# First row tiles of a routed feed-forward loaded before the last four scatter sends

## What is computed

```python
normed = layernorm(x) * ln_gamma + ln_beta
probs = softmax(normed @ router_w.T)            # 8 experts
top_v, top_i = top_k(probs, 2)
gates = softmax(top_v)
for e in range(8):                              # swiglu, 128 -> 384 -> 128
    out += comb[:, e] * swiglu(normed, gate_up_w[e], down_w[e])
out += swiglu(normed, shared_gate_up_w, shared_down_w)
x = x + tanh(g_ffn[1]) * out
```

## Time and profile before

| | |
|---|---|
| median of 3 runs | 318.86 us (317.61 to 321.77) |
| the profiled execution's own time | 318.32 us |
| its span in the trace | 316.4 us |
| instructions | 7622 |
| PE busy | 273.7 us (87%) |
| DVE busy | 231.8 us (73%) |
| ACT busy | 207.7 us (66%) |
| POOL busy | 155.1 us (49%) |
| mean granted PE clock | 0.951 of full |

### The profile page before, as it was taken

The page is one execution under the profiler, slowest core; times in us unless marked ns, Lnnn a source line. Parts: engine busy times, 40 slices in busy tenths (PEclk is TensorE's granted clock), DMA queues, the critical chain, the costliest instruction groups (busy, mean ns, idle before and its releaser), DMA issues.

```text
span 316.4 us, 7622 instructions
## 1 busy us (share of the span) xinstructions
PE 273.7 (87%) x2454; PEld 207.2 (65%) x2454; DVE 231.8 (73%) x702; ACT 207.7 (66%) x481; POOL 155.1 (49%) x202
## 2 busy tenths in 40 slices
PE   8787996896999896999888763969899999999995
PEld 4463352455677554687666651348799999999995
DVE  4468178956987755788989967899577777777765
ACT  2765599986577678976864743534577777878530
POOL 2524289023632628625022778781027888888700
PEclk9899999999999999999999955589999999999999
DMA  7790002100349999980000111113212222201074
GB/s 210 228 362 39 1 2 85 48 3 0 134 151 190 182 189 182 190 130 0 2 1 11 35 36 43 51 51 84 57 52 79 71 77 70 68 32 37 8 233 135
DMA packets 34613, 28.13 MB, mean 89 GB/s; under 512 B 3072, under 2 KB 32389, under 8 KB 33936
## 3 DMA queue, kind: packets, MB, share of 16 engines
q1 hardware_dynamic: 32192, 23.77, 33.6%
q0 software_dynamic: 2240, 3.72, 3.6%
q10 hardware_dynamic: 144, 0.15, 0.2%
HBM read 14.15 MB, written 14.40 MB: 90 GB/s over the span
## 4 chain that ended last, share of the span: by engine, by line
PE 33%; DVE 22%; issue 14%; ACT 12%; POOL 12%; DMA 4%; SPq 1%; POOLq 0%; DVEq 0%; ACTq 0%
PE bank L1201 29%; POOL expert_rows L850 11%; ACT w_high L559 2%; ACT w_scaled L557 2%; DMA wr<-in 2%; DVE bn_raw L867 1%; DVE nm L998 1%; DVE region_k L1000 1%; DVE region_x L1160 1%; DMA region_q<-expert_rows 1%; ACT x_hat L547 1%; DVE x L899 1%; PE bank L1425 1%; DVE region_k L966 1%; ACT x_hat L671 1%
## 5 line engine op out<-in xcount | busy, mean ns | idle before, releaser
L1185 DVE TENSOR_TENSOR region_k<-region_x,region_k 128x768 f16<-128x768 f32 (+1 forms) x33 | 30.6, 927 | 21.6 <-ACT region_k L721 21.6
L1201 PE MATMUL bank<-w_scaled,w_high 128*128 128x256 f16 x252 | 42.4, 273 | 0.1
L1201 PE MATMUL bank<-w_high,region_k 128*128 (+1 forms) x380 | 37.6, 220 | 3.3 <-DVE x L1175 2.5
L850 POOL DMA_INDIRECT expert_rows<-region_k,slot_dest x22 | 27.1, 1232 | 26.4 <-DVE region_k L1172 19.1
L824 POOL DMA_INDIRECT dispatched_rows<-region_t,slot x28 | 29.0, 1036 | 16.1 <-issue 8.3
L721 ACT ACTIVATE region_k<-region_x 128x768 f16<-128x768 f32 (+1 forms) x33 | 26.8, 812 | 14.2 <-DVE region_x L1160 14.2
L1201 PE MATMUL bank<-w_scaled,w_low 128*128 128x256 f16 x126 | 34.3, 273 | 0.0
L1201 PE MATMUL bank<-w_low,region_k 128*128 (+1 forms) x190 | 33.8, 220 | 0.0
L1201 PEld LDWEIGHTS bank<-w_high,region_k 128*128 128x128 f16 x380 | 30.8, 98 | 4.5 <-issue 4.1
L1160 DVE SCALAR_TENSOR_TENSOR region_x<-bank,region_w 128x768 f32<-128x768 f32 (+1 forms) x33 | 30.4, 921 | 3.2 <-ACT region_w L726 2.1
L1201 PE MATMUL bank<-filler 128*128 128x512 f16 x94 | 27.9, 418 | 3.9 <-DVE region_k L909 2.4
(11 more groups left out here) (246 smaller groups left out, 755.5 us busy)
## 6 DMA issues: line engine op xcount, KB each, us to landing
dispatched_rows<-pad_rows SPq DMA_DIRECT2D x8, 1048.0 KB, 18.4
w_scaled<-in SPq DMA_DIRECT2D x5, 1024.0 KB, 7.8
w_scaled<-dispatched_rows SPq DMA_DIRECT2D x21, 131.0 KB, 2.2
region_q<-expert_rows SPq DMA_DIRECT2D x3, 512.0 KB, 5.1
x<-in SPq DMA_DIRECT2D x4, 256.0 KB, 3.9
region_w<-in SPq DMA_DIRECT2D x2, 512.0 KB, 7.0
out<-x SPq DMA_DIRECT2D x3, 256.0 KB, 2.8
w_scaled<-in SPq DMA_DIRECT2D x1, 704.0 KB, 4.0
```

The source lines that it names most:

```text
L850: pool.indirect_dma_start(ytok, bass.IndirectOffsetOnAxis(dst[:, n, h:h + 1].bitcast(U32), 0), yv[n % 4][:, h * D:(h + 1) * D], None, boun ...
L1185: dve.tensor_tensor(hsplit[:, v, k:2 * k], hid[:, v, 0:k], hsplit[:, v, 0:k], ALU.subtract).then_inc(hidden_low, 1)
L1201: return pe.matmul(o, l, r, start=start, stop=stop)
```

## The change

- The list of steps has 2 dense steps before the rows and 6 behind them. There are still 33 steps and 21 row tiles; the first rows step is s = 6.
- Row tiles 0 to 7 are the first 256 slots of expert 0 to 7, with fixed addresses and fixed weights. Only tiles 8 to 20 come from the table, which has 16 entries in place of 32.
- SP's first load waits for the sends of the first 12 token tiles (24 sends). The last four sends count on a semaphore of their own, `last_sent`. DVE writes per expert 2 where fewer than 256 rows had come from those 12 tiles, else 1. SP reads this value into a register ahead of the loads of tiles 0 to 7 and waits for `rows_needed` to reach it. POOL raises `rows_needed` to 2 once the last four have landed.
- `tiles_numbered`, `tiles_placed` and `windows_packed` move from DVE's iterations before 0, 1 and 2 to those of rows steps 1, 2 and 3 (s = 7, 8, 9); `gates_of_all` moves from iteration 3 to 2.
- Down products of steps 1 and 3 use bank 6, so down(s) waits one add less up to s = 4. Bank 6 is also where rows are turned, so PE's late iteration waits for add(3) before it turns tile 0; it no longer waits for the packed table.
- `slot_dest(n)` moves from two iterations ahead to the end of the step's own iteration, behind low.

```diff
-TTAB = 4 * ROUNDS + 8
-AHEAD = 2
+LISTED = TILES - E
+ROUNDS = -(-LISTED // 8)
+TTAB = 8 * ROUNDS
-DENSE_FIRST = 3
+DENSE_FIRST = 2
+DOWN_IN_6 = (1, 3)
+LAST_SENDS = 16 * 2 * (NS - GROUPS[SPARSE - 1][0])
...
-            eng.wait_ge(tiles, 1)
-            rows = [eng.value_load(trow_i[0:1, n:n + 1], min_val=0, max_val=E * REG) for n in range(AHEAD)]
             eng.wait_ge(w_low_done, CHUNKS)
-            eng.wait_ge(sent, 16 * 2 * NS)
+            eng.wait_ge(sent, 16 * 2 * GROUPS[SPARSE - 1][0])
+            eng.wait_ge(rows_needed, 1)
             for n in range(TILES):
                 wait(eng, rows_turned, n - 3)
                 wait(eng, dest_ready, n - 3)
-                row = rows[n] if n < AHEAD else eng.value_load(trow_i[0:1, n:n + 1], min_val=0, max_val=E * REG)
+                if n < E:
+                    eng.wait_ge(rows_needed, eng.value_load(needi[0:1, n:n + 1], min_val=1, max_val=2))
+                elif n == E:
+                    eng.wait_ge(rows_needed, 2)
+                    eng.wait_ge(tiles, 2)
+                row = n * REG if n < E else eng.value_load(trow_i[0:1, n - E:n - E + 1], min_val=0, max_val=E * REG)
...
+            pool.wait_ge(rows_needed, 1)
+            pool.wait_ge(last_sent, LAST_SENDS)
+            pool.memset(all_sent[:, :], 1.0).then_inc(rows_needed, 1)
...
             def tiles_counted():
                 dve.wait_ge(counts_made, 1)
-                link(dve.tensor_copy(cnt[:, :], bank[6][:, 0:E]))
-                link(dve.tensor_scalar(cnti[:, :], cnt[:, :], float(TP - 1), None, ALU.add))
+                link(dve.tensor_scalar(need[:, :], bank[6][:, 0:E], float(TP), 1.0, ALU.is_lt, ALU.add))
+                dve.tensor_copy(needi[:, :], need[:, :]).then_inc(rows_needed, 1)
+                dve.tensor_copy(cnt[:, :], bank[6][:, E:2 * E]).then_inc(tiles, 1)
...
-            after_hidden = {0: top2_apart, 1: tiles_placed, 2: windows_packed, 3: gates_of_all}
+            after_hidden = {0: top2_apart, 2: gates_of_all, STEP_OF[1]: tiles_numbered, STEP_OF[2]: tiles_placed, STEP_OF[3]: windows_packed}
...
-                ahead = STEPS[s + 2] if s + 2 < len(STEPS) else ("", 0)
-                if ahead[0] == "rows" and ahead[1] >= 2:
-                    slot_dest(ahead[1])
...
-                if ahead[0] == "rows" and ahead[1] < 2:
-                    slot_dest(ahead[1])
+                if s < len(STEPS) and STEPS[s][0] == "rows":
+                    slot_dest(STEPS[s][1])
...
                 pe.wait_ge(hidden_low, s + 1)
-                wait(pe, rows_ready, s)
+                if s == DOWN_IN_6[0]:
+                    pe.wait_ge(tiles, 1)
+                wait(pe, rows_ready, s - 1 if s <= DOWN_IN_6[-1] + 1 else s)
...
                 if late:
-                    pe.wait_ge(tiles, 2)
-                    load_window(0)
-                    e = experts()
-                    load_window(1)
+                    pe.wait_ge(rows_ready, DOWN_IN_6[-1] + 1)
                     turn(0)
                     down(s - 1, None)
```

More of the change, by code:

```diff
@@ L276, in build @@
         cnti = sb("count_i", [P, E], I32)
+        need = sb("sends_needed", [P, E])
+        needi = sb("sends_needed_i", [P, E], I32)
+        all_sent = sb("all_sent", [P, 1])
         ntil = sb("tiles_of", [P, E])
@@ L425, in build @@
         sent = sem("sent")
+        last_sent = sem("last_sent")
+        rows_needed = sem("rows_needed")
         router_split = sem("router_split")
@@ L464, in build, with down_bank @@
         SUM_BANK = 3 - gate_up_bank(len(STEPS) - 1)
+        def down_bank(s):
+            return bank[6] if s in DOWN_IN_6 else bank[7]
         def wait(eng, s, v):
@@ L824, in send_rows @@
                         pool.indirect_dma_start(disp, bass.IndirectOffsetOnAxis(slot[:, t, c:c + 1].bitcast(U32), 0),
-                                                pay[:, t, :], None).then_inc(sent, 16)
+                                                pay[:, t, :], None).then_inc(sent if t < GROUPS[SPARSE - 1][0] else last_sent, 16)
             for stage, t in skewed(NT, C_EVERY, C_POOL, C_POOL_AT):
@@ L1074, in tiles_counted, with tiles_numbered @@
                 dve.wait_ge(counts_made, 1)
-                link(dve.tensor_copy(cnt[:, :], bank[6][:, 0:E]))
-                link(dve.tensor_scalar(cnti[:, :], cnt[:, :], float(TP - 1), None, ALU.add))
+                link(dve.tensor_scalar(need[:, :], bank[6][:, 0:E], float(TP), 1.0, ALU.is_lt, ALU.add))
+                dve.tensor_copy(needi[:, :], need[:, :]).then_inc(rows_needed, 1)
+                dve.tensor_copy(cnt[:, :], bank[6][:, E:2 * E]).then_inc(tiles, 1)
+            def tiles_numbered():
+                dve.wait_ge(tiles, 1)
+                link(dve.tensor_scalar(cnti[:, :], cnt[:, :], -1.0, 0.0, ALU.add, ALU.max))
                 link(dve.tensor_scalar(cnti[:, :], cnti[:, :], 8, None, ALU.logical_shift_right))
@@ L1088, in tiles_placed @@
                 dve.tensor_scalar(trow_i[:, :], trow[:, :], float(E * REG), None, ALU.min).then_inc(tiles, 1)
[L1090 to L1095, removed]
+                link(dve.tensor_scalar(tw[:, :, :], te[:, :].rearrange("p (i j) -> p i j", j=8), float(E - 1), None, ALU.min))
                 link(dve.tensor_tensor(tw[:, :, :], tw[:, :, :],
@@ L1174, in _ @@
                         xf32 = x[:, n * T:(n + 1) * T, :].rearrange("p t d -> p (t d)")
-                        dve.scalar_tensor_tensor(xf32, bank[7][:, :], tgw[:, :], xf32, ALU.mult, ALU.add).then_inc(rows_ready, 1)
+                        dve.scalar_tensor_tensor(xf32, down_bank(s - 2)[:, :], tgw[:, :], xf32, ALU.mult, ALU.add).then_inc(rows_ready, 1)
                     else:
@@ L1178, in _ @@
                         for u in range(DT):
-                            last = dve.scalar_tensor_tensor(x[:, NS + u, :], bank[7][:, u * D:(u + 1) * D], comb[:, u, n:n + 1],
+                            last = dve.scalar_tensor_tensor(x[:, NS + u, :], down_bank(s - 2)[:, u * D:(u + 1) * D], comb[:, u, n:n + 1],
                                                             x[:, NS + u, :], ALU.mult, ALU.add)
@@ L1476, in _ @@
                     if g == SPARSE - 1:
-                        mm(bank[6][:, 0:E], one, base[:, SPARSE, :]).then_inc(counts_made, 1)
+                        mm(bank[6][:, 0:2 * E], one, base[:, SPARSE - 1:SPARSE + 1, :].rearrange("p g e -> p (g e)")).then_inc(counts_made, 1)
             pe.wait_ge(w_low_done, CHUNKS)
@@ L1489, in experts, with of_expert @@
                 return [(word >> (3 * j)) & (E - 1) for j in range(8)]
+            def of_expert(v, expert, c, n):
+                return v[:, expert, c:c + n] if isinstance(expert, int) else v[:, ds(expert, 1), c:c + n].rearrange("p e n -> p (e n)")
             def turn(n):
@@ L1504, in gate_up @@
                 if kind == "rows":
-                    w = [[v[:, ds(expert, 1), i * P:(i + 1) * P].rearrange("p e n -> p (e n)") for v in gu_w] for i in range(NF)]
+                    w = [[of_expert(v, expert, i * P, P) for v in gu_w] for i in range(NF)]
                     pe.wait_ge(rows_turned_out, n + 1)
@@ L1537, in down @@
                 if kind == "rows":
-                    w = [[v[:, ds(expert, 1), i * D:(i + 1) * D].rearrange("p e n -> p (e n)") for v in dn_w] for i in range(FC)]
+                    w = [[of_expert(v, expert, i * D, D) for v in dn_w] for i in range(FC)]
                 elif kind == "dense":
@@ L1572, in expert_of @@
                     return None
-                return e[n % 4] if n // 4 == n_window else before[n % 4]
+                if n < E:
+                    return n
+                return e[n % 8] if n // 8 == n_window else before[n % 8]
             n_window = 0
@@ L1587, in _ @@
                     n = STEPS[s + 1][1]
[L1588 to L1591, removed]
+                    if n == E - 1:
+                        pe.wait_ge(tiles, 3)
+                        load_window(0)
+                    elif n >= E and n % 8 == 0:
+                        before, e, n_window = e, experts(), n // 8
+                        if n // 8 < ROUNDS:
+                            load_window(n // 8)
                 if ahead[0] == "rows" and ahead[1] > 0 and not late:
```

9 lines of the change are left out of this document (5 added, 4 removed).

## The result

Over 20 runs each the changed kernel took 320.98 us (318.45 to 324.77) and the kernel before 320.19 us (316.77 to 322.56), both medians. The ratio of the changed kernel to the one before is 1.0061, with a 95% interval of 1.0031 to 1.0090: about 1.9 us slower (1.0 to 2.9). The two medians are only 0.79 us apart; the ratio is the measure with an interval. The prediction said 318.0 us, 0.3 us faster than its reference run, with a range up to 320.6. It was wrong in the sign, and the time lies 0.4 us above the range. Its sum stood on one execution of the kernel before, of 318.32 us; in this measurement that kernel itself had a median of 320.19, 1.9 us more. So the time alone is outside by that shift too, and the sign is what has to be explained.

The account below looks back on a forecast made before the run. PE was taken as the bound, busy 35.00 of 35.00 us from 250 to 285 us. The terms -2.1 - 0.3 + 0.4 + 0.3 + 1.4 = -0.3 us on 318.32 us gave 318.0 us, range 315.5 to 320.6.

Parts of the forecast that it names:

- The walk to the first rows step: New order up to the first rows step's gate_up: start at 217.70, not 222.80, gaining 2.1 us after a 2.97 dense step.
- The 2.49 us before down(1): PE's idle time up to 210.00, waiting for an add of DVE; claimed to go.
- The wait that I said would take their place: Before tile 0 is turned, PE idles 3.1 us until 216.50, because add(3) must first read bank 6.
- my margin of 1.8 us: Before the first turn: the first load was to land by 214.7, ahead of add(3), which frees PE at 216.50.
- (a): Table work on DVE at s = 7, 8, 9, ahead of the add PE's next down needs: 0.4 us lost.
- (b): `slot_dest` behind low in rows steps: later loads, 0.5 us of slack before the turn; 0.3 us lost, bounds 0 and 4.1.
- the rival's own bound: Rival that the load ring bounds the rows steps: worst landings on 17 ring-fed tiles cost 4.1 us, 321.8; chance 0.13.
- (c): Fixed weights for eight tiles: gains nothing, since PE's register work is hidden already.
- (d): Result rows read back a dense step earlier against PE: the 0.32 us wait at the end goes.
- (e): PE's clock falls to 1.2 GHz after the 3.1 us idle before the first turn: 1.4 us lost, bounds 0 and 1.7.

Follow-up runs that it names:

- e9: e1 with SP's register reads ahead of the ring waits and the gate arithmetic moved behind add(3), ahead of low(5): ratio 0.9885 to the kernel before.
- e1: The changed kernel with `slot_dest` moved back to two iterations ahead of its step: ratio 0.9929 to the kernel before.
- e3: The kernel before with one edit, `slot_dest` behind low of its own step: ratio 1.0149 to the kernel before.
- e2: The changed kernel with five load buffers in place of four, `slot_dest` left behind low: ratio 0.9998 to the kernel before.
- e5: e1 with SP's first load waiting until all 28 sends have landed: ratio 1.0064 to the kernel before.
- e6: e4 with SP's first load waiting until all 28 sends have landed: ratio 1.0018 to the kernel before.
- e8: The changed kernel with SP's register read ahead of the two ring waits, `slot_dest` left behind low: ratio 1.0011 to the kernel before.
- e10: e4 with SP's register reads moved ahead of the ring waits: ratio 0.9914 to the kernel before.
- e7: The kernel before with only the down products of steps 1 and 3 in bank 6, and the wait for add(3): ratio 1.0017 to the kernel before.
- e4: e1 with three dense steps ahead of the rows, as in the kernel before: ratio 0.9951 to the kernel before.

## Why the prediction was wrong, point by point

**The walk to the first rows step: right in size.** Forecast a start 5.1 us earlier, or 2.1 with the dense step paid back; measured 5.49 and 2.5. Some 0.4 us of that is the clock, which rose sooner in this execution (hid(1) came 4.99 us into the feed-forward, before 5.39). The 2.49 us before down(1) were gone. The wait that I said would take their place came with the forecast size, 3.06 us for 3.1. A wait of 0.97 us before down(2) was not in the walk; it cost nothing, since PE had to wait again at the turn.

**Who ends that wait: half wrong.** I named add(3), with the first load in 1.8 us earlier. The load was issued at 215.34 and landed 2.8 us later, 218.1; add(3) was out at 218.04. I had 212.5 and 2.2, to which the 2.2 us of the later start are to be added. Of my margin of 1.8 us 0.6 went in a later issue, 0.6 in a slower landing and 0.5 in an add(3) that came sooner than walked. It cost 0.2 us at most in this kernel, and in e9 the landing alone sets the turn.

**(a) The table work: right in size.** Forecast 0.4; in e1, where no landing disturbs, its two long intervals lose 0.07 and 0.20.

**(b) `slot_dest` behind low: the step that failed.** The term was 0.3 us; it measured 4.5 (e1 beside the changed kernel) and 3.6 (e3 beside the kernel before). The edit leaves 2.7 us of the 11.4 between a load's issue and its turn. That geometry was right: ready 2.8 us after the turn, issue 0.79 later, the tile needed 6.38 after the turn, about 0.5 us of slack on a landing of 2.2 to 2.4. What failed was the distribution of landings, taken from 17 loads of one execution whose worst was 3.2 (one of the other 16 took 2.5, not 2.4 or less). In the changed kernel three loads took 3.8 to 4.0, in e3 one took 4.3. One such landing with 0.5 us of slack stops PE for about a microsecond, and some 0.4 more are lost around the stop. The four stops (3.06 us), with 0.17 more in each of their intervals and 0.21 in each of the three intervals behind them, make 4.4 of the 4.5 us. With the rival's own bound (4.1) in hand I gave it 0.13.

**(c), (d): right.** The fixed weights gained nothing that shows; the end gained 0.34 us. The third load came at 219.6, as forecast for the later start.

**(e) The clock: wrong in this execution, open in general.** I charged 1.4 us for a fall behind the 3.1 us of idle time. In the changed kernel's profile the clock stayed at full. It fell behind idle stretches of 2.49 (before), 3.11, 2.48, 6.66, 4.11, 2.92 and 2.29 us (e2, e3, e5, e6, e8, e10), and behind 1.35 and 1.33 in e7, and did not behind 3.06, 3.20, 1.84 and 2.09 (changed, e1, e4, e9). Near this size the length of the idle stretch alone does not tell which it will be, and it should have been a term of about half its price. That the fall stayed away was luck of this execution, and it hid 1.4 us of the forecast cost.

**Corrected sum**: with e1's values for (a) and (b), -2.5 - 0.3 + 0.3 + 4.5 - 0 = +2.0 us. The two profiles themselves give -5.49 + 2.97 up to gate_up of tile 0, -0.34 behind the last turn and, from the second turn on, 63.43 against 58.87 us, 4.56 more for (a) and (b) together: +1.70, the 1.69 us of the two feed-forwards. The ratio says 1.9.

The Trainium skill's floor of 600 ns for a register load (DMA: Bandwidth & Descriptors, Latency and other measured facts), which I set aside for the trace's 0.27 us, describes something that the ring does pay: e8 took the read out and the way from `slot_dest` to issue fell by 0.57 us. The engine's record of the load alone is 0.27; with the operations on the register behind it the path is twice that. I had this in the sum already, within the 0.79, and not as a lever; so the estimate that the page's figure would leave only 0.2 us of slack counted a part of it twice.

## What to carry to other kernels

A buffer is free only when its last reader is done, so a small operation that reads it belongs as early as its data allow; moved behind the big ones it holds the buffer and takes the slack from the next load. Compare the slack of a load ring with the slowest landings of many executions, not with the median of one: here 0.5 us of slack lost 4.5 us over 21 loads, 0.57 us more won most of it back in one execution, and the old place of the operation, with 11.4 us from issue to turn, took landings of 4.4 us without a stop. Keep addresses and flags read ahead of the wait, and put scalar bookkeeping where the engine waits anyway.

## What had not been expected of the hardware

- Landings of the same 131 KB load took 2.1 to 2.5 us mostly. In nine of the twelve profiles one or more took 3.1 to 4.4; the slowest that the traces of e5, e8 and e9 show are 2.9, 2.9 and 3.0. What makes the long ones long was not found.
- SP took 0.79 us from the end of the operation it waited for to the issue of a load when a register read stood between, and 0.22 us without.
- The turn behind a stop of PE took 0.43 us to the next product where 0.22 is usual.
- The clock fell or stayed at much the same idle time (3.11 us: fell; 3.20 us: stayed).
